# Spiking steps: the sign-turned membrane on VectorE, the spike tiles on GpSimd, and the stage's loops written out

## What is computed

```python
h = jnp.square(jax.nn.relu(jnp.einsum('bsd,fd->bsf', x, W_fc)))
y = jnp.einsum('bsf,df->bsd', h, W_proj)

def step(mem, _):
    reset = jax.lax.stop_gradient(spike_fn(mem - THRESHOLD))
    mem_new = BETA * mem + y - reset * THRESHOLD
    spk = spike_fn(mem_new - THRESHOLD)
    return (mem_new, spk)
mem0 = jnp.zeros_like(y)
_, spks = jax.lax.scan(step, mem0, None, length=NUM_STEPS)
return jnp.sum(spks, axis=0) / NUM_STEPS
```

## Time and profile before

| | |
|---|---|
| median of three runs | 1602.4 us (1601.57 to 1603.79) |
| the profiled execution | 1600.68 us |
| its span | 1599.1 us |
| busy over the span | TensorE 1447.5, its weight loads 1200.0, VectorE 1088.4, ScalarE 902.2, GpSimd 623.2 us |
| mean granted TensorE clock | 0.968 of full speed |
| the spiking stage | from about 1445 us of the span to its end |

### The profile page before, as it was taken

How to read it: one execution, slowest core, us unless ns; L and a number is a source line. 1 busy time by engine, 2 the same in 40 slices (tenths; PEclk the granted TensorE clock), 3 DMA queues, 4 the chain that set the end, 5 groups by cost and what they waited for, 6 DMA issues and landing times. The chain is left out here.

```text
span 1599.1 us, 27379 instructions
## 1 busy us (share of the span) xinstructions
PE 1447.5 (91%) x9078; PEld 1200.0 (75%) x9094; DVE 1088.4 (68%) x2356; ACT 902.2 (56%) x1903; POOL 623.2 (39%) x747
## 2 busy tenths in 40 slices
PE   6999999999999996559789999899989999987996
PEld 4888888888888875229767878787878787766884
DVE  5676776776777776898655757575656566774886
ACT  3666666666666653660155656565656565545662
POOL 1233434334334333840113333333433342445885
PEclk9999999999999998899899999999999999998998
DMA  8544444444444422000064444444444444320111
GB/s 260 176 157 133 140 153 131 160 130 153 133 154 130 151 77 78 25 0 0 18 202 134 133 131 131 133 131 136 133 129 133 135 124 135 106 68 1 33 33 40
DMA packets 198329, 182.27 MB, mean 114 GB/s; under 512 B 14144, under 2 KB 195392, under 8 KB 198208
## 3 DMA queue, kind: packets, MB, share of 16 engines
q1 hardware_dynamic: 197632, 180.60, 35.9%
q10 hardware_dynamic: 576, 0.13, 0.0%
HBM read 95.43 MB, written 84.93 MB: 113 GB/s over the span
## 5 line engine op out<-in xcount | busy, mean ns | idle before, releaser
L911 POOL TENSOR_TENSOR PN<-E,RC 128x512 f32<-128x512 f32 (+1 forms) x384 | 336.3, 904 | 581.7 <-DVE RC L869 581.7
L823 DVE TENSOR_REDUCE MX<-pS 128x6 f32<-128x462 f32 (+1 forms) x384 | 221.9, 578 | 256.2 <-PE pS L573 256.0
L608 PE MATMUL pO<-work,PT 128*128 128x128 f32 (+1 forms) x2560 | 333.9, 278 | 15.9 <-ACT PT L711 15.9
L662 ACT ACTIVATE G<-pP 128x308 f32<-128x308 f32 (+1 forms) x488 | 209.0, 429 | 244.8 <-PE pP L514 244.4
L608 PEld LDWEIGHTS pO<-work,PT 128*128 128x128 f32 (+1 forms) x2560 | 312.4, 194 | 23.0 <-issue 20.5
L573 PE MATMUL pS<-G,XT 128*128 128x462 f32 (+1 forms) x768 | 324.4, 507 | 0.0
L702 ACT ACTIVATE E<-E 128x462 f32<-128x462 f32 (+1 forms) x384 | 209.6, 546 | 151.0 <-DVE E L833 142.3
L512 PE MATMUL pP<-Chi,Ahi 128*128 128x308 f32 x496 | 240.4, 485 | 1.4 <-ACT G L662 1.2
L593 PE MATMUL pT<-ident,PN 128*128 128x128 f32 (+1 forms) x1280 | 203.8, 278 | 32.7 <-POOL PN L911 31.7
L833 DVE TENSOR_TENSOR E<-pS,MX 128x462 f32<-128x462 f32 (+1 forms) x384 | 223.6, 582 | 9.1 <-issue 0.2
L711 ACT ACTIVATE PT<-pT 128x512 f32<-128x512 f32 (+1 forms) x384 | 200.5, 523 | 47.4 <-PE pT L593 47.3
(11 more groups left out here) (194 smaller groups left out, 1948.7 us busy)
## 6 DMA issues: line engine op xcount, KB each, us to landing
values<-ST SPq DMA_DIRECT2D x256, 256.0 KB
work<-values SPq DMA_DIRECT2D x512, 128.0 KB
values<-ST SPq DMA_DIRECT2D x64, 208.0 KB
work<-values SPq DMA_DIRECT2D x128, 104.0 KB
C<-in_ctx SPq DMA_DIRECT2D x32, 154.0 KB
out<-s_O SPq DMA_DIRECT2D x16, 256.0 KB, 2.3
work<-in_L_xattn_Wq SPq DMA_DIRECT2D x2, 512.0 KB, 7.5
work<-in_L_xattn_Wkv SPq DMA_DIRECT2D x2, 512.0 KB, 8.0
```

Of the source, the lines that this page charges most:

```text
L608: last = nc.tensor.matmul(pO[:, 0:CH], PT[0:rows, c, :], V[(t - 1) % VRING][0:rows, tile, CH * hh:CH * hh + CH], start=c == 0, stop=c == C ...
L662: return nc.scalar.activation(G[0:live, g % 2, :, head, :], bank[0:live, 0:KEYCOLS].rearrange("p (b k) -> p b k", k=KEYS), ACT.Copy)
L823: nc.vector.tensor_reduce(MX[:, h0:h1], pS[u][:, 0:(h1 - h0) * KEYS].rearrange("p (h k) -> p h k", k=KEYS), X_AXIS, ALU.max).then_inc(max_ ...
L911: nc.gpsimd.tensor_tensor(out, e, scale, ALU.mult).then_inc(prob_ready, 1)
```

## The change

A stage k of a group is now two instructions on VectorE, and one on GpSimd to which nothing on VectorE's path is due at once. VectorE keeps the membrane with its sign turned, NEG = -mem, in two buffers for each parity. LEAK is 0.9 mem + pY as before (for k > 0 as -0.9 NEG + pY), and then, with a wait for its own LEAK, one more scalar_tensor_tensor makes the next NEG = (mem > 1) - LEAK (for k > 0 as (NEG < -1) - LEAK). GpSimd makes the spike tile from Y or NEG by a tensor_scalar, five for each group, and no MEM. VectorE's stage 4 falls away, GpSimd has a fifth operation at a group's end. NEG of stage k waits until the spike tile of stage k - 1 has been made, since it overwrites the buffer which that one reads. The copy Y waits for the first NEG of the group two before instead of its first LEAK. The loops of all engines are written out, so that semaphore values and addresses are constants.

```diff
-        MEM = [sb(f"MEM{i}", [128, 512]) for i in range(2)]
+        NEG = [[sb(f"NEG{i}{k}", [128, 512]) for k in range(2)] for i in range(2)]
...
-        def run(engine, step):
-
-            for half in range(2):
-                step(half, half, 0)
-            with engine.Fori(1, LOOPED) as i:
-                for half in range(2):
-                    step(i * 2 + half, half, i)
-            for i in range(LOOPED, GROUPS // 2):
-                for half in range(2):
-                    step(2 * i + half, half, i)
+        def run(step):
+
+            for g in range(GROUPS):
+                step(g, g % 2, g // 2)
...
@@ ScalarE @@
-                    act.wait_ge(leaked[half], i * LATER + (1 - LATER))
+                    act.wait_ge(mem_done[half], i * LATER + (1 - LATER))
...
@@ VectorE, stage(g, half, i, k) @@
                 if k == 0:
                     dve.wait_ge(y_out, g + 1)
-                    mem = Y[half]
+                    if has(g, -2):
+                        dve.wait_ge(mem_done[half], i * LATER)
+                        dve.wait_ge(spiked[half], i * STEPS)
+                    mem, decay, above, limit = Y[half], BETA, ALU.is_gt, THRESHOLD
                 else:
                     dve.wait_ge(mem_done[half], i * LATER + k)
-                    mem = MEM[half]
-                if k < LATER:
-                    nc.vector.scalar_tensor_tensor(out=LEAK[half][:, :], in0=mem[:, :], scalar=BETA,
-                                                   in1=pY[half][:, :], op0=ALU.mult, op1=ALU.add
-                                                   ).then_inc(leaked[half], 1)
-                if k == 0 and has(g, -2):
-                    dve.wait_ge(counted, g - 1)
-                nc.vector.tensor_scalar(SPK[:, half, k, :], mem[:, :], THRESHOLD, None, ALU.is_gt
-                                        ).then_inc(spiked[half], 1)
+                    mem, decay, above, limit = NEG[half][k % 2], -BETA, ALU.is_lt, -THRESHOLD
+                nc.vector.scalar_tensor_tensor(out=LEAK[half][:, :], in0=mem[:, :], scalar=decay,
+                                               in1=pY[half][:, :], op0=ALU.mult, op1=ALU.add
+                                               ).then_inc(leaked[half], 1)
+                dve.wait_ge(leaked[half], i * LATER + (k + 1))
+                if k > 0:
+                    dve.wait_ge(spiked[half], i * STEPS + k)
+                nc.vector.scalar_tensor_tensor(out=NEG[half][(k + 1) % 2][:, :], in0=mem[:, :], scalar=limit,
+                                               in1=LEAK[half][:, :], op0=above, op1=ALU.subtract
+                                               ).then_inc(mem_done[half], 1)
...
@@ GpSimd @@
-            def reset(g, half, i, k):
-
-                pool.wait_ge(leaked[half], i * LATER + (k + 1))
-                pool.wait_ge(spiked[half], i * STEPS + (k + 1))
-                nc.gpsimd.tensor_tensor(MEM[half][:, :], LEAK[half][:, :], SPK[:, half, k, :],
-                                        ALU.subtract).then_inc(mem_done[half], 1)
+            def spike(g, half, i, k):
+
+                if k == 0:
+                    pool.wait_ge(y_out, g + 1)
+                    if has(g, -2):
+                        pool.wait_ge(counted, g - 1)
+                    nc.gpsimd.tensor_scalar(SPK[:, half, k, :], Y[half][:, :], THRESHOLD, None, ALU.is_gt
+                                            ).then_inc(spiked[half], 1)
+                else:
+                    pool.wait_ge(mem_done[half], i * LATER + k)
+                    nc.gpsimd.tensor_scalar(SPK[:, half, k, :], NEG[half][k % 2][:, :], -THRESHOLD, None, ALU.is_lt
+                                            ).then_inc(spiked[half], 1)
```

More of the change, by code:

```diff
@@ L1365, in spiking_ffn @@
         LATER = STEPS - 1
-        AHEAD = 4
-        LOOPED = (GROUPS - AHEAD) // 2
-        def run(engine, step):
-            for half in range(2):
-                step(half, half, 0)
-            with engine.Fori(1, LOOPED) as i:
-                for half in range(2):
-                    step(i * 2 + half, half, i)
-            for i in range(LOOPED, GROUPS // 2):
-                for half in range(2):
-                    step(2 * i + half, half, i)
+        def run(step):
+            for g in range(GROUPS):
+                step(g, g % 2, g // 2)
         def has(g, n):
@@ L1392, in step @@
                              O[half][:, :, :]).then_inc(stored[half], 16)
-            run(sp, step)
+            run(step)
             for half in range(2):
@@ L1452, in step @@
                     turn(g + 3)
-            run(pe, step)
+            run(step)
             count(GROUPS - 2, 0, GROUPS // 2 - 1)
@@ L1499, in step @@
                     x_hi(g + 3, 1 - half)
-            run(act, step)
+            run(step)
         @block.vector
@@ L1551, in step @@
                 stage(g, half, i, 1)
-                if has(g, -1):
-                    stage(g + (-1), 1 - half, before, 4)
                 stage(g, half, i, 2)
@@ L1556, in step @@
                     x_lo(g + 3, 1 - half)
-            run(dve, step)
+            run(step)
             last = GROUPS // 2 - 1
             stage(GROUPS - 1, 1, last, 3)
-            stage(GROUPS - 1, 1, last, 4)
             store(GROUPS - 2, 0, last)
@@ L1592, in step @@
                 before = i if half else i + (-1)
-                reset(g, half, i, 0)
+                spike(g, half, i, 0)
                 if has(g, -1):
-                    reset(g + (-1), 1 - half, before, 3)
-                reset(g, half, i, 1)
+                    spike(g + (-1), 1 - half, before, 4)
+                spike(g, half, i, 1)
                 if has(g, 4):
                     centre(g + 4)
-                reset(g, half, i, 2)
+                spike(g, half, i, 2)
                 if has(g, 4):
                     normalise(g + 4)
-            run(pool, step)
-            reset(GROUPS - 1, 1, GROUPS // 2 - 1, 3)
+                spike(g, half, i, 3)
+            run(step)
+            spike(GROUPS - 1, 1, GROUPS // 2 - 1, 4)
 def program(nc, a, out):
```

## The result

| | before | changed |
|---|---|---|
| median | 1601.99 us (1599.57 to 1603.79, 4 runs) | 1629.28 us (1627.94 to 1631.62, 4 runs) |
| span of the profiled execution | 1599.1 us | 1628.7 us |
| spiking stage, from its first XC to the end | 153.7 us | 180.3 us |
| steps of groups 3 to 13, mean | 8.08 us | 10.78 us |
| group 15's Y to the end of the last O | 16.1 us | 15.05 us |

The ratio is 1.0173, with a 95% interval of 1.0155 to 1.0191: 27 us slower, where 5.7 us faster had been forecast and 1606 was the range's upper end. Of the 26.6 us that the stage grew by, the ten steps between the Y of group 3 and that of group 13 hold 27.1; the end of the program became 1.1 us shorter.

A forecast was written before the change was run, and what follows sets the result against it. TensorE was taken to bound the spiking stage's steady part, at 7.85 us a step without gaps. Steps -2.3 and -0.7, last pY products +0.7 and drain -3.4 gave -5.7: 1602.4 to 1596.7 us, range 1594 to 1606.

The forecast's parts named there:

- T = 0.75: Duration in us of one spike tile on GpSimd, one input and bf16 output, five a step; no row had it.
- Rival A: Slow GpSimd spike tile delays each NEG and lengthens VectorE's step: 1613 us at a tile of 1.15; chance 0.18.
- GpSimd's side of the exclusion: GpSimd operations held up by VectorE's NEG: no time given, GpSimd's step put at 5.8 us.
- VectorE's side: NEG held up by GpSimd's XC, XN and fresh Y's spike: about 0.8 us, making VectorE's step 7.3.
- rival C: TensorE's 0.23 us a step doesn't come back, from ScalarE, late Xlo or slower spike tiles: 1599.7 us; chance 0.10.
- (a): Spiking steps 3 to 13 fall from 8.08 to 7.85 us, -2.3; the step from group 2 to 3, -0.7.
- (b): Last products into pY start later, a NEG standing before group 13's last LEAK: some +0.7 us.
- (c): Drain from group 15's Y to the end: 12.7 us against 16.1, so -3.4.
- Rival B: GpSimd doesn't hold NEG up at all, VectorE's step is 6.5 us: -6.7, 1595.7 us; chance 0.17.
- D: Longer written-out code stalls the engines' instruction fetch; 0.6 us lost in each of twelve steps would erase the gain; chance 0.03.

The follow-up runs named there:

- the run of single operations: The kernel before with ten GpSimd forms added behind its last result, other engines idle: the comparison took 1.494 us, a copy 0.61.
- half tiles: The changed kernel with GpSimd's spike tiles made on 256 of 512 columns, the others cleared once: 1597.30 us, 0.9970 of before.
- the copy run: The changed kernel with GpSimd's comparison replaced by a plain copy of the membrane into the bf16 tile: 1599.35 us, 0.9994 of before.

## Why the prediction was wrong

**The step that failed: T = 0.75, "the line of one input plus that 0.11, since the new operation has one input".** It measured 1.49 alone, twice the value and above the upper bound of 1.15, which was taken from the two-input MEM. The number of inputs was the wrong measure of nearness. Nor does the figure that the prediction quotes beside it from the Trainium skill (GPSIMD Engine Reference, "3.1 Elementwise — side-by-side cycle accounting"), 769 ns measured at 512 elements, hold for this form: over as many columns it takes nearly twice that. The rows that were read, a cast and a select that stood on one line, hold for those operations alone; the run of single operations has the copy at 0.61, as that line says (0.64), and every tensor_scalar of one operation at 1.49. The select looked like proof that the operation with a scalar is quick as well, and was one row of 128 columns. The kernel before had no GpSimd tensor_scalar at all, so the honest upper end was open.

**Rival A had the right cause, and put it on the wrong engine.** It said that the slow tile makes VectorE's step 7.3 + 4 x (T - 0.73). With 1.49 that is 10.3, and 10.64 was measured, but this nearness is luck: the engine that binds is GpSimd with 5 x 1.47 + 2.0 + 1.33, and the price was given for T up to 1.15 only. The run with half tiles does not bear the formula out: with 0.85, the tile alone, it gives less than TensorE's 7.85, and so no test; with 1.07, the tile in place, it gives 8.7, where 7.85 was measured.

**GpSimd's side of the exclusion was put at nothing.** The prediction had seen it, an XN of 1.23 for 1.04 beside a spike tile, and yet gave GpSimd 5 x 0.75 + 2 x 1.04 = 5.8 us a step with no time for being held. In the changed kernel it is 1.33 a step. With half tiles the same sum gives 5 x 0.85 + 2.1 = 6.3, and GpSimd was busy for 7.7 of 7.85.

**VectorE's side was taken the right way and priced too low.** NEG is held up and does 0.55 us afterwards (0.48 was taken), and NEG itself takes 0.69, not 0.62. What XC and XN cost it was put at 0.8 us a step; with a quick tile it was 1.6 (the copy run), and the steps were 8.25 instead of 7.85, 4 us in ten. So the forecast would not have been safe with T = 0.75 either: the half tile, 0.85 alone, came out 3.8 us below before (some 6.0 without the clearing), the copy, 0.62, only 1.8 below (1599.35 against 1601.17), and the sum has no term that tells these apart. The copy's time is that of rival C (1599.7), by another cause than C's.

**(a), the steps, -2.3 - 0.7:** the place of the gap was read rightly, TensorE waits for Xlo, and a spike tile held up by XN stands in front of it; but neither needs the new division. With the loops alone written out the steps are 7.85, and all those tiles are still on VectorE. "I cost it at 0" was said of the loops, and they are the whole -2.3. The first full step, from group 2 to 3, is another matter: from Y to Y it is 8.41 us before and with the loops written out, 7.93 with half tiles and 7.85 with the copy, so there the new division gives some -0.5.

**(b), +0.7:** about right where the tile is quick: the step from Y of group 14 to that of 15 was 6.19 before, 6.69 with half tiles: +0.5. **(c), -3.4:** right too where the tile is quick (12.5 against 12.7). In the changed kernel GpSimd's queue of spike tiles stands in the end as well, and it is 15.05, only 1.1 less than before.

Rival B (no exclusion) is out by the NEG of 1.45 inside XC, which takes 0.69 when it reads only one tile from SBUF. D (straight-line code stalls) is out by the run with the loops alone. Profiles of single executions place the start of the stage between 1443.7 and 1449.4 us in kernels whose code ahead of it is the same and which add nothing at its start; what moves it was not looked into, so differences of 1 or 2 us are read from the medians and from the stage's own steps.

## What to carry to other kernels

Before work goes to an engine that the kernel does not use for that form of instruction, time the very form by itself on the chip: a copy, a comparison with a scalar and a subtraction of two tiles differ by up to 2.4 times on GpSimd here, and not in the order of their inputs. Then count all engines' steps against the one that binds, with the time in which two of them hold each other up, and put the new work where there is slack: here ScalarE was busy for only 54.8 of 84 us, and two tiles there with three on GpSimd, the loops written out, gained 8.7 us, where five on GpSimd lost 27. An unrolled loop and a moved instruction in one change should be timed apart; here the unrolling seems to be a gain by itself, some 2.9 us of the stage.

## What the runs showed that was not expected

- A tensor_scalar of GpSimd over 128x512 takes 1.49 us with a comparison or a multiplication, to f32 or bf16, 1.93 with two operations, and so more than a tensor_tensor (1.15 to 1.26).
- XC and the spike tile hold a NEG up in different ways. Behind XC, NEG ends 0.55 us after XC's end. A NEG issued 0.13 us after a spike tile's start (1529.16 against 1529.03) ends 1.02 us later, at 1530.18, 0.3 us before that tile does: it seems to be held for the tile's first 0.5 or 0.6 us only, and the tile is not stretched (1.49). What it waits for in it was not tried.
- A quicker GpSimd tile was worse than a slower one: 8.25 us a step with 0.62 (the copy), 7.85 with the half tile's 1.07 (0.85 alone), through the places that XC and XN take beside NEG.
